# Sparse tiles and row length at the end of a patch top-k kernel: ten sparse tiles in place of six, dense halves moved a patch at a time

## The reference

```
xn    = groupnorm(x, 32 groups, eps 1e-5)             # no affine part
s     = 0.5 * (|dx xn| + |dy xn|) + 0.5 * |xn|        # dx, dy: [-1, 0, 1], zero padding
score = mean of s over each 32 x 32 patch             # per image, channel and patch
mask  = 1 for the 128 of 256 channels with the largest score, for each patch
out   = x + xn * mask
```

## Time and profile before

| | us |
|---|---|
| time, median of 3 runs (lowest, highest) | 2055.26 (2054.36, 2056.93) |
| the profiled execution's own time | 2053.4 |
| its span in the trace | 2051.6 |

### The profile page before, as it was taken

The page is one execution under the profiler, slowest core; times in us unless marked ns, Lnnn a source line. Parts: engine busy times, 40 slices in busy tenths (PEclk is TensorE's granted clock), DMA queues, the critical chain, the costliest instruction groups (busy, mean ns, idle before and its releaser), DMA issues.

```text
span 2051.6 us, 16270 instructions
## 1 busy us (share of the span) xinstructions
PE 1373.3 (67%) x3528; PEld 674.0 (33%) x3528; DVE 1537.1 (75%) x2113; ACT 1593.2 (78%) x2405; POOL 1402.4 (68%) x975
## 2 busy tenths in 40 slices
PE   5899899786777777777767776877677777600000
PEld 2444444333333333433333333433333333300000
DVE  7988887888778787899787878888877787652210
ACT  4999999897898889998888898898888988730123
POOL 7999999677676667767766676767666766531226
PEclk9999999888988888988888888989888888855555
DMA  5898775199999999999999999999999999699995
GB/s 246 338 358 338 305 317 206 62 368 428 429 430 433 433 429 431 404 383 422 430 431 435 427 432 431 383 396 423 432 432 429 432 432 425 251 382 428 425 423 178
DMA packets 53672, 780.53 MB, mean 380 GB/s; under 512 B 11175, under 2 KB 11175, under 8 KB 16240
## 3 DMA queue, kind: packets, MB, share of 16 engines
q1 hardware_dynamic: 42096, 759.19, 88.1%
q0 software_dynamic: 11520, 20.77, 2.8%
HBM read 532.68 MB, written 293.60 MB: 403 GB/s over the span
## 4 chain that ended last, share of the span: by engine, by line
DMA 44%; ACT 16%; issue 11%; PE 8%; DVE 7%; another core or an unknown queue 6%; POOL 3%; DVEq 2%; SPq 1%; ACTq 1%; POOLq 0%
DMA again<-in_x_dram 41%; ACT again L706 8%; PE vertical L610 4%; PE vertical L612 4%; ACT thrown L764 3%; DVE stats L807 3%; DMA out_dram<-ring,pair 2%; DVEq L798 2%; ACT vertical L758 2%; ACT ring L724 1%; DVE largest L1000 1%; DMA ring<-in_x_dram 1%; SPq L464 1%; DVE vertical L821 1%
## 5 line engine op out<-in xcount | busy, mean ns | idle before, releaser
L610 PE MATMUL vertical<-ring,plus 128*128 128x512 f32 (+1 forms) x1200 | 667.1, 641 | 304.5 <-ACT vertical L758 304.0
L299 POOL TENSOR_TENSOR pair<-ring 128x960 f32<-128x960 f32 x360 | 638.2, 1793 | 30.5 <-DVE scratch L978 21.9
L612 PE MATMUL vertical<-ring,minus 128*128 128x512 f32 (+1 forms) x1200 | 633.3, 612 | 0.0
L807 DVE BATCH_NORM_STATS2 stats<-ring 128x6 f32<-128x512 f32 x960 | 582.2, 677 | 25.5 <-DMA ring<-in_x_dram 14.9
L764 ACT ACTIVATE thrown<-ring,record 128x1024 bf16<-128x1024 f32 x480 | 548.2, 1142 | 8.8
L706 ACT ACTIVATE again<-again,coef 128x1024 f32<-128x1024 f32 x360 | 416.1, 1227 | 165.7 <-DMA again<-in_x_dram 165.7
L834 DVE TENSOR_REDUCE sums<-pair 128x2 f32<-128x1920 f32 (+1 forms) x212 | 454.8, 2145 | 84.7 <-POOL pair L299 84.0
L305 POOL TENSOR_TENSOR pair<-ring 128x960 f32<-128x960 f32 x120 | 269.3, 2244 | 296.2 <-DVE sums L834 272.0
L610 PEld LDWEIGHTS vertical<-ring,plus 128*128 128x128 f32 x1200 | 240.7, 212 | 578.2 <-ACT vertical L758 364.9
L612 PEld LDWEIGHTS vertical<-ring,minus 128*128 128x128 f32 x1200 | 250.7, 209 | 296.2 <-issue 296.2
L758 ACT ACTIVATE vertical<-vertical 128x960 f32<-128x960 f32 x320 | 303.6, 949 | 24.7 <-PE vertical L612 24.7
(11 more groups left out here) (108 smaller groups left out, 1245.0 us busy)
## 6 DMA issues: line engine op xcount, KB each, us to landing
ring<-in_x_dram SPq DMA_DIRECT2D x59, 4096.0 KB, 23.3
again<-in_x_dram SPq DMA_DIRECT2D x98, 2048.0 KB, 15.5
out_dram<-again SPq DMA_DIRECT2D x98, 2048.0 KB, 14.9
out_dram<-kept SPq DMA_DIRECT2D x12, 2048.0 KB, 11.3
kept<-in_x_dram SPq DMA_DIRECT2D x4, 4096.0 KB, 23.5
out_dram<-ring SPq DMA_DIRECT2D x6, 2048.0 KB, 32.7
kept<-in_x_dram SPq DMA_DIRECT2D x4, 2048.0 KB, 26.5
ring<-in_x_dram SPq DMA_DIRECT2D x4, 2048.0 KB, 28.0
```

Source lines behind the costliest of these rows:

```text
L299: return nc.gpsimd.tensor_tensor(part.rearrange("p (r c) -> p r c", r=PATCH), xs[:, w, :, 2:], xs[:, w, :, 0:PATCH - 2], ALU.subtract)
L610: nc.tensor.matmul(v[:, first:end], plus[:], xs[:, first + 2 * PATCH:end + 2 * PATCH], start=True, stop=False)
L612: done = nc.tensor.matmul(v[:, first:end], minus[:], xs[:, first:end], start=False, stop=True)
L807: nc.vector.bn_stats(stats[:, k, :], buffer[:, k * BN:(k + 1) * BN])
```

## The change

Sparse tiles become 4 to 13 (ten instead of six), five pairs instead of three: 12 and 13, 4 and 5, 6 and 7, 8 and 9, 10 and 11. Four more tiles are copied during image 0; their copies stand behind the last four loads of that image. The dense halves become 12 (tiles 15, 14, 0 to 3). Each dense half is stored as four DMAs of one patch column (128 rows of 4 KB, 512 KB), each as soon as DVE has finished that column, and loaded as four such DMAs; DVE still waits for all four of them.

```diff
-SPARSE_FIRST, SPARSE_END = 8, LAST - 1
+SPARSE_FIRST, SPARSE_END = 4, LAST - 1
...
             for u in range(RING + 1):
                 load_ahead(0, LOOPED - 1, u)
+                copy_tile(base + SPARSE_END - RING - 1 + u)
...
             def store_dense(n):
-                t, half = DENSE[n]
-                sp.wait_ge(dense_finished, n + 1)
-                store_half(base + t, half, dense_slots[n % DENSE_SLOTS], dense_stored[n % DENSE_SLOTS])
+                for j in range(HALF_COLS):
+                    part, tile, pixels = patch_of_half(n, j)
+                    sp.wait_ge(dense_finished, HALF_COLS * n + j + 1)
+                    sp.dma_start(out[tile, :, pixels], part).then_inc(dense_stored[n % DENSE_SLOTS], 16)
...
             def load_dense(n):
...
+                sp.wait_ge(dense_stored[n % DENSE_SLOTS], 16 * HALF_COLS * (n // DENSE_SLOTS))
+                for j in range(HALF_COLS):
+                    part, tile, pixels = patch_of_half(n, j)
+                    sp.dma_start(part, x[tile, :, pixels]).then_inc(dense_loaded[n % DENSE_SLOTS], 16)
```

More of the change, by code:

```diff
@@ L69 @@
 DENSE_SLOTS, DENSE_LAG = 7, 2
-assert SPARSE_PAIRS[0] == (LAST - RING, LAST - RING + 1) and SPARSE == 2 * (LOOPED - 2)
+assert SPARSE_PAIRS[0] == (LAST - RING, LAST - RING + 1) and SPARSE == 2 * (LOOPED - 2) + RING + 1
 OUT_FIRST, OUT_LOOPED, OUT_LAST, OUT_RANKING = (0, 2, 2), (2, 2, 2), (2, 2, 2, 0), 2
@@ L553, in _, with patch_of_half @@
             image_loads(IMAGES - 1, True)
+            def patch_of_half(n, j):
+                t, half = DENSE[n]
+                first = half * HALF + j * AREA
+                return dense_slots[n % DENSE_SLOTS][:, j * AREA:(j + 1) * AREA], base + t, slice(first, first + AREA)
             def store_dense(n):
-                t, half = DENSE[n]
-                sp.wait_ge(dense_finished, n + 1)
-                store_half(base + t, half, dense_slots[n % DENSE_SLOTS], dense_stored[n % DENSE_SLOTS])
+                for j in range(HALF_COLS):
+                    part, tile, pixels = patch_of_half(n, j)
+                    sp.wait_ge(dense_finished, HALF_COLS * n + j + 1)
+                    sp.dma_start(out[tile, :, pixels], part).then_inc(dense_stored[n % DENSE_SLOTS], 16)
             def load_dense(n):
[L561 to L565, removed]
+                sp.wait_ge(dense_stored[n % DENSE_SLOTS], 16 * HALF_COLS * (n // DENSE_SLOTS))
+                for j in range(HALF_COLS):
+                    part, tile, pixels = patch_of_half(n, j)
+                    sp.dma_start(part, x[tile, :, pixels]).then_inc(dense_loaded[n % DENSE_SLOTS], 16)
             for n in range(len(DENSE)):
@@ L572, in _ @@
             for slot in range(DENSE_SLOTS):
-                sp.wait_ge(dense_stored[slot], 16 * len(range(slot, len(DENSE), DENSE_SLOTS)))
+                sp.wait_ge(dense_stored[slot], 16 * HALF_COLS * len(range(slot, len(DENSE), DENSE_SLOTS)))
             for slot in range(SLOTS):
@@ L1064, in finish_dense @@
                     v = pixels[:, j * AREA:(j + 1) * AREA]
-                    done = nc.vector.tensor_scalar(v, v, coef[:, t, 0, w:w + 1], coef[:, t, 1, w:w + 1],
-                                                   ALU.mult, ALU.add)
-                done.then_inc(dense_finished, 1)
+                    nc.vector.tensor_scalar(v, v, coef[:, t, 0, w:w + 1], coef[:, t, 1, w:w + 1],
+                                            ALU.mult, ALU.add).then_inc(dense_finished, 1)
             loads = 2 * LOOPED * (IMAGES - 1)
@@ L1073, in _ @@
                 elif n >= DENSE_SLOTS:
-                    dve.wait_ge(dense_loaded[n % DENSE_SLOTS], 16 * (n // DENSE_SLOTS))
+                    dve.wait_ge(dense_loaded[n % DENSE_SLOTS], 16 * HALF_COLS * (n // DENSE_SLOTS))
                 finish_dense(n)
```

## The result

| | before | after |
|---|---|---|
| time, median of 5 runs (lowest, highest), us | 2055.18 (2053.63, 2056.93) | 2043.93 (2043.52, 2045.02) |
| span of the profiled execution, us | 2051.6 | 2041.1 |
| predicted time, us | | 2042.7 (range 2027 to 2059) |

The ratio of the times is 0.9947, 95% interval 0.9933 to 0.9962: 11.3 us faster, where 12.6 was forecast.

What follows compares the result with a forecast made beforehand. The last stage was taken as bound first by full DMA engines shared by two queues, then by POOL's issue pace. The q0 chain ends at 1947.4 + 82.4 + 9.2 = 2039.0, 12.6 us less: 2042.7 us, range 2027 to 2059.

Steps and rivals of the forecast that it cites:

- copies in image 0: End of image 0: four added copies, 12.0 us of queue each, leave late transfers 3 us early, costing 0 us.
- bytes q0 to q1 in the shared part: Last stage while both queues share full DMA engines: packets alternate, so q0 gets 1/3 of the rate instead of 1/9.
- rate in the shared part: Last stage, both queues together: 377 GB/s for the first 27 us, 400 behind them, taken as 393.
- unit 2 landed: Sparse chain on q0: the second 2.1 MB scatter unit lands at 1840, its data having started at 1808.
- a unit of q0: Sparse chain, shared part: 2.10 MB scattered or gathered (8 x 128 rows, half skipped) takes 16.0 us at 131 GB/s.
- from the last issue's end to the span's end: End of the last stage: the span runs on 9.2 us behind POOL's last scatter, as before the change.
- SP's issue of a DMA: Dense queue q1, 68 DMAs instead of 33: 0.4 us of SP's time each, hidden behind the transfers.
- 136 us on top of 1940: Dense queue: by the skill's 2.0 us fixed cost per DMA, 136 us more, shared part ending near 2060; the prediction rejected this.
- 1 (half of the bytes): Last stage: q0 gets half the bytes, 10.7 us a unit, time 2009; chance 0.08.
- 2 (q0 keeps its ninth): Last stage: q0 stays at 47 GB/s, POOL then sets the pace, time 2064; chance 0.12.
- 3 (copies that hold up image 0): End of image 0: copies of 24.2 us each delay it by 16.6 us, time 2059; chance 0.10.
- 4 (4 KB rows are slow): Last stage: 4 KB rows of both queues move at 350 GB/s, 18.0 us a unit, time 2059; chance 0.08.

Runs made afterwards that it cites:

- a: Changed kernel's ten sparse tiles, but dense halves moved whole in 16 KB rows: 2070.39 us, ratio 1.0080 to the kernel before.
- d: Ten sparse tiles as in the changed kernel, dense halves in eight DMAs of 2 KB rows: 2009.47 us, ratio 0.9783 to the kernel before.
- e: Ten sparse tiles as in the changed kernel, dense halves in two DMAs of 8 KB rows: 2058.38 us, ratio 1.0018 to the kernel before.
- f: Changed kernel with eight instead of four copies behind image 0's last four loads: 2064.92 us, ratio 1.0058 to the kernel before.
- g: Changed kernel without the dense side of the last image, sparse side whole: one run of 1998.34 us.
- k: Changed kernel with dense DMAs of the same number and size, but 32 partitions of 16 KB rows each: 2102.78 us, ratio 1.0242 to the kernel before.
- c: Eight sparse tiles instead of the changed kernel's ten, dense halves in 4 KB rows: 2029.11 us, ratio 0.9877 to the kernel before.
- b: Six sparse tiles as in the kernel before, dense halves in the change's 4 KB rows: 2032.52 us, ratio 0.9897 to the kernel before.
- j: Changed kernel with no row skipped, so unselected patches are gathered and scattered too: one run of 2087.88 us.
- m: Eight sparse tiles instead of the changed kernel's ten, dense halves in 2 KB rows: 2021.7 us, ratio 0.9842 to the kernel before.

## Why the prediction was right

| step | predicted | measured |
|---|---|---|
| copies in image 0 | 0 us | 0 us (coefficients at 1802.57, before 1803.09) |
| bytes q0 to q1 in the shared part | 1 to 2 | 11.14 to 21.93 MB |
| rate in the shared part | 393 GB/s | 354 to 385 at first, then 409 to 415; 401 from 1808 to 1940 |
| first gather issued | 1828 | 1827.78 |
| unit 2 landed | 1840 | 1846.0 |
| a unit of q0 | 16.0 us | 15.9 us (units 3 to 8) |
| dense side ends | 1940 | 1936 to 1941, dying away |
| last waited-for scatter | 1937.1 | 1942.36 |
| two turns at POOL's pace | 82.4 us | 1952.5 to 2034.5, 82.0 us |
| from the last issue's end to the span's end | 9.2 us | 6.6 us |
| span | 2039.0 | 2041.1 |

The mechanism held at each step, and the experiments show that it is the mechanism and not the bytes: with ten sparse tiles and the same bytes, rows of 16, 8, 4 and 2 KB gave 2070, 2058, 2044 and 2009 us (spans of the profiles 2064, 2057, 2041 and 2008).

Three terms were off, and they partly cancelled, so that 2043.9 lies so near to 2042.7 is in part luck.

The first is the landing of the first two units, 38 us behind q0's first data at 1808 and not 32. I had put the low rate of that stretch into one mean (I wrote 393; its own parts, 27 us at 377 and 105 us at 400, give 395) and spread it over all units. But the rate explains only 1 us of the 6. The row of q0 from 1804 to 1846, when the second unit had landed:

```profile
q0 software_dynamic: 2611, 4.69, 31.1%
```

A unit has 1152 packets (20736 for 18 units), so two have 2304, and q0 was already 307 packets, some 4 us, into the next ones. A unit lands later than q0's mean progress says. The prediction had no term for this lag. That some DMA engines run ahead of others would do it, and the slow dying away of q1 from 1936 to 1941 fits, but no row here tells the engines apart, so that is not shown.

The second is the rate behind them. At 409 to 415 GB/s a third is 137 to 138 GB/s, and a unit would take 15.2 us; the landings lay 15.9 us apart, as the lag grew, from 261 packets at unit 3 to 407 at unit 7. So the 16.0 of the prediction was met by a rate taken too low and a lag left out.

The third is the end: 6.6 us instead of 9.2. This stretch took 6.6 us in a, d, e, f, g, k and the changed kernel, 9.2 before and 11.8 in c; the difference lies in the silent part behind the last transfer, and its cause stays open. So 2.6 of the 10.5 us between the two profiles are not the change's mechanism as far as I can show it, and the mechanism's own gain in the profiles is 7.9 us, against 12.6 forecast.

Two terms that changed nothing in the sum were wrong too. SP's issue of a DMA took 1.3 to 1.75 us in the median and not 0.4, and SP issued without a pause from 1803.94 to 1922.4; that this stayed hidden is seen from the full DMA engines only. And 136 us on top of 1940 would have been 2076, not 2060; the second load landed 9.7 us behind the first, since it was issued 0.4 us later, which still is its bytes' time alone.

Of the rivals: 1 (half of the bytes) did not come with this row length, but it is what d is at 2 KB, and its estimated time, 2009, is d's. 2 (q0 keeps its ninth) is refuted by the packets; its size of damage was about right: a, which has just that share, took 2070 where it said 2064, and e, at the 1/5 for which its walk gave a span of 2059, had 2056.8. 3 (copies that hold up image 0) was absent; by the walk, which f bears out, 3 us were left. 4 (4 KB rows are slow): refuted by b's 420 GB/s.

What the prediction did not ask is whether both parts of the change pull the same way. They don't: short rows with the old six tiles give 2032.5, ten tiles with long rows 2070.4, both together 2043.9. At 4 KB rows the four added sparse tiles cost 11 us, because behind the dense side POOL is alone with them for 92 us while the DMA engines are half idle.

## What to carry to other kernels

When two DMA queues share full engines, as SP's queue and POOL's indirect one do here, count packets, not bytes: the queue with the shorter rows, or with skipped rows, gets the smaller share, and the other queue's row length is the knob. Work out what each side needs when left alone (here POOL's 1.28 us for each indirect DMA, 185 us in all, and the bytes at 400 GB/s) and choose rows and split so that both end together; with 2 KB rows this kernel ran 2.2% below the one before. A transfer moved into idle time is free only as far as the next load behind it in the same queue has slack.

## What the runs showed of the hardware

- A packet of q0 whose row is skipped takes a turn like any other (equal counts within 3 packets before, after and in a, b, c, e and k with skipped rows, and in j without).
- The time of one packet of each queue, together, grew with their bytes: 0.614 us for 16.4 KB before (88 us x 16 engines / 2294), 0.213 us for 5.5 KB after (80 x 16 / 6020), so about 0.037 us a KB and 0.01 us on top. The straight line through these two gives 0.345 us for e and 0.28 us for j (7.3 KB); measured 0.346 (40 x 16 / 1850) and 0.280 (60 x 16 / 3431). It doesn't hold for k's DMAs over 32 partitions: 0.574 us (40 x 16 / 1115) for 12.7 KB, where it gives 0.48.
- SP's issue of a DMA took 0.34 us where few were outstanding; in the changed kernel the median was 1.3 to 1.75 us, with rows here of one group of stores and one of loads (ns, min/median/max), and up to 5 us, as if the issue waited for room in the queue. It cost nothing, since the queue was full then.

```profile
L566 SPq DMA_DIRECT2D out_dram<-again x16: 1152/1750/2067, 1836.4 to 1920.5; - x16
L572 SPq DMA_DIRECT2D again<-in_x_dram x4: 476/1408/5080, 1874.1 to 1877.6; - x4
```

- Where POOL's scatters ended last, the span ran on behind the last transfer without any activity for 4.7 to 4.9 us (a, d, e, f, g, j, k and the changed kernel), 7.4 us before and 10 us in c. Where the dense side ended last, it was under 1 us (b, whose last transfer was at 2030.5 of 2031.3 us, and m, 2019.2 of 2019.7). A comparison of two kernels within 5 us should look there first.
- A queue that runs dry does so slowly: b's q1 alone moved 420 GB/s until 2020, then 330 until 2025 and 110 to the end; m as shown above.
- DMAs over 32 partitions of 16 KB rows moved 256 to 354 GB/s at a full DMA share (k), where 128 partitions moved 427.
